# Mixture of experts after an adaptive layer norm, on one core: how the expert rows come back into token order

## The chip, the cores and the metric

The kernel runs on one core of a Trainium2 chip. The metric is the device time of one execution in microseconds (us), the median of several runs. Its engines are named as the profile names them: PE is TensorE (PEld its weight loads), DVE is VectorE, ACT is ScalarE, POOL is GpSimd and SP is SyncE; SPq, ACTq and POOLq are their sequencers, which issue DMAs.

## The reference, cut to what matters

The input x has 8 batches of 128 tokens with 128 features, float32. An adapter and a layer norm, chosen for each batch by a language number, make n from x. A router picks one of 8 experts for each of the 1024 tokens; the expert's result and that of a shared network are added to x:

```python
x0 = x
n = _L0_cond_ref(x, ids, W1, b1, W2, b2, gamma, beta)     # adapter, layer norm
logits = n @ router_w.T
top_idx, score = argmax(logits), sigmoid(max(logits))
xs = n * score[:, None]
h = silu(xs @ expert_gate[e]) * (xs @ expert_up[e])       # for each expert e, FF = 256
moe_out = sum over e of onehot[:, e] * (h @ expert_down[e])
sh = silu(n @ shared_gate) * (n @ shared_up) @ shared_down
out = x0 + moe_out + sh
```

## The kernel before, in words

Everything is float32 and tokens lie in tiles of 128 rows, one row per partition. The work runs in three stages, each engine with its own program, tied by semaphores.

First stage: adapter, layer norm and router over the 8 batches in two groups of 4. VectorE works out for each token a slot in a list that is sorted by expert (`find_slot`, line 854). Each expert has one home tile of 128 places, and 7 more tiles take what runs over; of these the first four (`RARE = 4`) are always worked on, the last three only if the data needs them (`rare_in_use`, line 183), which is not so with these inputs. ScalarE scales the rows by their score (line 642), and GpSimd scatters them with eight indirect DMAs, one per batch (line 341), into the scratch `slots_x` in device memory: 129 numbers per row, the last one being the token's own number. That scratch was filled before with rows whose number is `NO_TOKEN = 4 * T`. SyncE then loads the sorted tiles back into `slot_x` with nine DMAs (line 268).

Second stage, beside it: the shared network. VectorE adds its result to x, batch by batch (`residual`, line 798), which gives `r_rows`. SyncE stores them to the output with two DMAs, each for four batches (line 272), on its queue behind the nine loads.

Third stage, twelve tiles (`main`: four run-over tiles, then the eight experts). For each tile TensorE transposes it (line 539), ScalarE copies it (line 683), TensorE multiplies with the expert's gate and up weights (line 547 for the run-over tiles, line 551 for the others), ScalarE applies silu (line 699), VectorE multiplies (line 944), TensorE multiplies with the down weights (line 575), and VectorE copies the result to `y` (line 949). For each tile GpSimd then issues an indirect DMA (line 350, in `tiles_out`) that adds its 128 rows to the output at the rows given by the token numbers (`compute_op=ALU.add`). The number `NO_TOKEN` of an unused place is above the bound `T - 1`, and its row is dropped (`bounds_check`, `oob_is_err=False`). Since these DMAs add to rows that the stores of line 272 write, GpSimd first waits for both stores (`r_out`). The program ends when SyncE has seen all of them land (`main.y_out`).

The order on every engine is the order of the code. GpSimd's descriptors for indirect DMAs go on the DMA queue named software_dynamic (q0), those of SyncE and ScalarE on queues named hardware_dynamic (q1 and q10).

Of the kernel before, what the change touches and what calls it, by code (L numbers as in the profile page):

```python
# [6 lines left out]
P = 128  # L7
F32 = mybir.dt.float32
# [9 lines left out]
def adaln_moe_kernel(nc, x, ids, w1rw, w2b2, lang_vecs, shared_w, expert_w, out):  # L18
# [3 lines left out]
    S, B, H = x.shape  # L22
# [5 lines left out]
    T = B * S  # L28
    assert S == P and H == P and shared_w.shape[1] == 2 * FF + K2 * H
    GROUPS = 2  # L30
    GB = B // GROUPS
# [13 lines left out]
    out_rows = out.rearrange("b s h -> (b s) h")  # L45

    with ExitStack() as ctx:  # L47
        def sb(name, shape, dt=F32):
            return ctx.enter_context(nc.sbuf_tensor(name, shape, dt))

        def sem(name):
            return ctx.enter_context(nc.semaphore(name))
# [74 lines left out]
        r_rows = sb("r_rows", [P, B, H])  # L127
# [5 lines left out]
        y = sb("y", [P, TILES, H])  # L133

# [23 lines left out]
        fill_x, x_out, r_out = sem("fill_x"), sem("x_out"), sem("r_out")  # L158

        sg_ps, su_ps, sg_done, hs_done = sem("sg_ps"), sem("su_ps"), sem("sg_done"), sem("hs_done")  # L160
        sd_ps, r_done = sem("sd_ps"), sem("r_done")
# [15 lines left out]
        rare = Run("rare", list(range(E + RARE, TILES)))  # L177
# [70 lines left out]

        block = ctx.enter_context(nc.Block())

        @block.sync
        def _(sp):
# [17 lines left out]
            for g in range(GROUPS):  # L270
                sp.wait_ge(r_done, (g + 1) * GB)
                sp.dma_start(out[g * GB:(g + 1) * GB].rearrange("b s h -> s b h"), r_rows[:, g * GB:(g + 1) * GB, :]
                             ).then_inc(r_out, 16)
# [3 lines left out]
            sp.wait_ge(main.y_out, 16 * main.n)  # L277

        @block.gpsimd
        def _(pool):  # L280
# [64 lines left out]
            def tiles_out(run):  # L345
                pool.wait_ge(r_out, 16 * GROUPS)
                for i, tile in enumerate(run.tiles):
                    pool.wait_ge(slot_x_in[piece_of(tile)], 16)
                    pool.wait_ge(run.y_done, i + 1)
                    nc.gpsimd.indirect_dma_start(  # L350
                        out=out_rows,
                        out_offset=bass.IndirectOffsetOnAxis(ap=slot_x[:, tile, H:H + 1].bitcast(U32), axis=0),
                        in_=y[:, tile, :], in_offset=None, bounds_check=T - 1, oob_is_err=False,
                        compute_op=ALU.add).then_inc(run.y_out, 16)
# [246 lines left out]
        def _(act):  # L601
# [102 lines left out]
            with nc.scalar.If(rare_in_use(nc.scalar)):  # L704
                expert_tiles(rare)
                act.wait_ge(rare.eh_done, rare.n)
            expert_tiles(main)

        @block.vector
        def _(dve):  # L710
# [248 lines left out]
            expert_tiles(main)  # L959

# [33 lines left out]
```

## Time and profile before

| | us |
|---|---|
| median of 3 runs | 69.2 (68.46 to 69.24) |
| the profiled execution's own time | 68.22 |
| its span, first to last instruction | 66.4 |
| POOL busy | 30.5 |
| PE busy | 48.8 |
| DVE busy | 27.0 |
| ACT busy | 22.7 |

The span is what the trace shows. The execution's own time has 1.82 us more, which lie outside it. The profile's busy time is an instruction's time on its engine; for an indirect DMA on POOL that is the time in which its descriptors are made, not the time in which its rows move. What a DMA takes from the start of its issue until it has landed stands in the rows "to landing". Times in the trace are counted in us from the start of the span.

### The profile page before, as it was taken

Reading aid. Unit: us, or ns where it says so; the run is one execution under the profiler, and the core shown is the slowest. Engines: PE = TensorE matmul, PEld = TensorE weight load, DVE = VectorE, ACT = ScalarE, POOL = GpSimd, SP = SyncE. Lnnn points to the kernel's source line nnn. Section 1 sums busy time; section 2 is a strip of 40 time slices with the busy share of each in tenths; the row PEclk is TensorE's granted clock in tenths of the full one; section 3 lists DMA queues with packets and bytes.
Section 4 is the critical chain, followed back from the end, with each engine's and each line's share of the span. In section 5 each row is a group of like instructions: output and inputs, shape, how many; then the busy total and the mean of one; then the engine's idle time right before and its main releaser. Section 6 shows DMA issues by size and latency. Waiting matters only on the chain.

```text
span 66.4 us, 1128 instructions
## 1 busy us (share of the span) xinstructions
PE 48.8 (74%) x312; PEld 36.4 (55%) x312; DVE 27.0 (41%) x119; ACT 22.7 (34%) x65; POOL 30.5 (46%) x51
## 2 busy tenths in 40 slices
PE   3999999999898967999629999999999840000000
PEld 1376888676647424479414469999999730000000
DVE  2602364576881789747500433353333530000000
ACT  0640256568778081330023555533344200000000
POOL 4002950000138658860000000898888888898820
PEclk9999999999999999999999999999999999855555
DMA  0870899999899841111269590043421003424140
GB/s 0 255 267 4 141 336 163 114 176 239 370 402 427 363 149 62 47 40 45 77 158 238 126 314 11 0 40 33 40 27 7 5 4 24 40 22 40 9 37 2
DMA packets 7994, 8.05 MB, mean 121 GB/s; under 512 B 1161, under 2 KB 7187, under 8 KB 7732
## 3 DMA queue, kind: packets, MB, share of 16 engines
q1 hardware_dynamic: 5820, 6.74, 38.2%
q0 software_dynamic: 1984, 1.06, 11.9%
q10 hardware_dynamic: 184, 0.18, 1.0%
q8 instruction: 3, 0.05, 0.3%
q14 instruction: 3, 0.02, 0.1%
HBM read 5.40 MB, written 2.83 MB: 124 GB/s over the span
## 4 chain that ended last, share of the span: by engine, by line
PE 52%; POOL 10%; ACT 9%; DVE 7%; issue 7%; DMA 7%; POOLq 3%; ACTq 0%
PE bank L551 11%; POOL out_dram L350 9%; PE bank L575 8%; PE bank L547 6%; PE bank L365 6%; DMA slots_x<-x_rows,slot 4%; PE bank L379 4%; PE bank L395 3%; PE bank L389 3%; POOLq L47 3%; ACT x_rows L642 3%; DMA slot_x<-slots_x 3%; PE bank L373 2%; PE bank L539 2%; ACT L663 2%
## 5 line engine op out<-in xcount | busy, mean ns | idle before, releaser
L350 POOL DMA_INDIRECT out_dram<-y,slot_x x12 | 18.8, 1564 | 15.1 <-DVE y L949 12.4
L341 POOL DMA_INDIRECT slots_x<-x_rows,slot x8 | 7.9, 990 | 4.2 <-ACT x_rows L642 1.8
L448 PE MATMUL bank<-nT,sh_w 128*128 128x512 f32 (+1 forms) x20 | 8.3, 527 | 0.9 <-DVE hs L793 0.9
L944 DVE TENSOR_TENSOR eh<-eg,bank 128x256 f32<-128x256 f32 x12 | 5.0, 418 | 9.1 <-ACT eg L699 9.1
L551 PE MATMUL bank<-exT,ex_w 128*128 128x128 f32 x64 | 8.5, 275 | 0.0
L551 PEld LDWEIGHTS bank<-exT,ex_w 128*128 128x128 f32 x64 | 7.8, 192 | 0.0
L699 ACT ACTIVATE eg<-bank 128x256 f32<-128x256 f32 x12 | 4.6, 383 | 9.0 <-PE bank L551 6.5
L949 DVE COPY y<-bank 128x128 f32<-128x128 f32 x12 | 3.4, 287 | 4.8 <-PE bank L575 4.8
L575 PE MATMUL bank<-ex_w,eh 128*128 128x128 f32 x32 | 5.0, 278 | 0.5 <-DVE eh L944 0.5
L683 ACT ACTIVATE exT<-bank 128x128 f32<-128x128 f32 x12 | 3.2, 273 | 5.8 <-PE bank L539 5.8
L365 PE MATMUL bank<-warm 128*128 128x512 bf16 x11 | 4.4, 538 | 1.1 <-DVE eps L712 1.1
L448 PEld LDWEIGHTS bank<-nT,sh_w 128*128 128x128 f32 x20 | 3.3, 190 | 2.9 <-DVE hs L793 1.6
L575 PEld LDWEIGHTS bank<-ex_w,eh 128*128 128x128 f32 x32 | 4.2, 192 | 0.7 <-DVE eh L944 0.7
L547 PE MATMUL bank<-ex_w,exT 128*128 x8 | 4.2, 618 | 0.3 <-ACT exT L683 0.3
L539 PE MATMUL bank<-ident,slot_x 128*128 128x128 f32 x12 | 3.2, 277 | 1.5 <-issue 1.5
L463 PEld LDWEIGHTS bank<-sh_w,hs 128*128 128x128 f32 x32 | 3.7, 192 | 0.5 <-issue 0.5
L333 POOL TENSOR_SCALAR score<-half_tanh 128x4 f32<-128x4 f32 x1 | 0.2, 192 | 8.1 <-ACT half_tanh L630 8.1
L463 PE MATMUL bank<-sh_w,hs 128*128 128x128 f32 x32 | 3.7, 275 | 0.0
L637 ACT ACTIVATE sg<-bank 128x512 f32<-128x512 f32 x4 | 2.4, 601 | 2.5 <-PE bank L448 2.5
L793 DVE TENSOR_TENSOR hs<-sg,bank 128x512 f32<-128x512 f32 x4 | 2.6, 682 | 1.2 <-PE bank L448 1.0
L610 ACT ACTIVATE hT<-bank,params 32x128 f32<-32x128 f32 x6 | 1.7, 347 | 3.9 <-PE bank L389 3.9
L642 ACT ACTIVATE x_rows<-bank,score 128x128 f32<-128x128 f32 x8 | 2.3, 368 | 2.1 <-DVE score L891 1.7
(125 smaller groups left out, 74.7 us busy)
## 6 DMA issues: line engine op xcount, KB each, us to landing
ex_w<-in_expert_w_dram SPq DMA_DIRECT2D x2, 1536.0 KB
slots_x<-empty_row SPq DMA_DIRECT2D x1, 967.5 KB, 11.3
slot_x<-slots_x SPq DMA_DIRECT2D x4, 129.0 KB, 3.8
x_tok<-in_x_dram SPq DMA_DIRECT2D x2, 256.0 KB, 3.6
out_dram<-r_rows SPq DMA_DIRECT2D x2, 256.0 KB, 3.2
sh_w<-in_shared_w_dram SPq DMA_DIRECT2D x1, 384.0 KB, 3.5
slot_x<-slots_x SPq DMA_DIRECT2D x4, 64.5 KB, 1.9
slot_x<-slots_x SPq DMA_DIRECT2D x1, 193.5 KB, 4.0
```

What stands on the lines that cost most here:

```text
L341: nc.gpsimd.indirect_dma_start(out=slots_x, out_offset=bass.IndirectOffsetOnAxis(ap=slot[:, b:b + 1], axis=0), in_=x_rows[:, b, :], in_off ...
L350: nc.gpsimd.indirect_dma_start(out=out_rows, out_offset=bass.IndirectOffsetOnAxis(ap=slot_x[:, tile, H:H + 1].bitcast(U32), axis=0), in_=y ...
L365: nc.tensor.matmul(bank[bk][:, 0:blocks * P], warm[:], warm[:].unsqueeze(1).to_broadcast([P, blocks, P]), start=True, stop=True)
L448: last = nc.tensor.matmul(bank[SH_BANKS[k][u]][:, first * S:end * S], sh_w[:, u * FF + k * P:u * FF + (k + 1) * P], nT[:, g * GB + first:g ...
L463: last = nc.tensor.matmul(sh_y_place(b), hs[:, k, b * S:(b + 1) * S], sh_w[:, 2 * FF + k * H:2 * FF + (k + 1) * H], start=(k == 0), stop=( ...
L539: nc.tensor.transpose(bank[EX_X[i % 2]][:, 0:P], slot_x[:, run.tiles[i], 0:H], ident[:]).then_inc(run.exT_ps, 1)
L547: last = nc.tensor.matmul(bank[EX_GU[i % 2]][:], exT[:, i % 2, :], ex_w[:, bass.ds(expert[i], 1), 0:2 * FF], start=True, stop=True)
L551: last = nc.tensor.matmul(bank[EX_GU[i % 2]][:, k * P:(k + 1) * P], ex_w[:, expert[i], k * P:(k + 1) * P], exT[:, i % 2, :], start=True, s ...
L575: last = nc.tensor.matmul(bank[EX_Y[i % 2]][:, 0:H], hidden, ex_w[:, bass.ds(expert[i], 1), 2 * FF + k * H:2 * FF + (k + 1) * H], start=(k ...
L642: nc.scalar.activation(x_rows[:, b, 0:H], bank[N_ROWS][:, (b % GB) * H:(b % GB + 1) * H], ACT.Copy, scale=score[:, b:b + 1]).then_inc(scal ...
L699: nc.scalar.activation(eg[:, i % 2, :], bank[EX_GU[i % 2]][:, 0:FF], ACT.Silu).then_inc(run.eg_done, 1)
L944: nc.vector.tensor_tensor(eh[:, i % 3, :], eg[:, i % 2, :], bank[EX_GU[i % 2]][:, FF:2 * FF], ALU.mult).then_inc(run.eh_done, 1)
```

## The change

The twelve indirect DMAs no longer add to the output: they write the expert rows plainly into a second scratch, `y_tok`, in token order. They keep the bound, and no longer wait for the stores of line 272, which are gone. When all twelve have landed, `y_tok` is loaded back into `y_back` by four plain DMAs of two batches each, the first and third from SyncE, the second and fourth from ScalarE. VectorE adds `y_back` to `r_rows` in four additions, and four plain DMAs, again by turns from SyncE and ScalarE, store the sums.

```diff
     slots_x = nc.dram_tensor("slots_x", (TILES * P, ROW), F32, kind="Internal").ap()
-    out_rows = out.rearrange("b s h -> (b s) h")
+    y_tok = nc.dram_tensor("y_tok", (T, H), F32, kind="Internal").ap()
+    RETURNS = 4
...
+        def batches(i):
+            return slice(i * B // RETURNS, (i + 1) * B // RETURNS)
+
+        def load_back(engine, i):
+            engine.dma_start(y_back[:, batches(i), :], y_tok.rearrange("(b s) h -> s b h", s=S)[:, batches(i), :]
+                             ).then_inc(y_in[i], 16)
+
+        def store_out(engine, i):
+            engine.wait_ge(out_added, i + 1)
+            engine.dma_start(out[batches(i)].rearrange("b s h -> s b h"), out_sb[:, batches(i), :]
+                             ).then_inc(out_stored, 16)
...
         def _(sp):
...
-            for g in range(GROUPS):
-                sp.wait_ge(r_done, (g + 1) * GB)
-                sp.dma_start(out[g * GB:(g + 1) * GB].rearrange("b s h -> s b h"), r_rows[:, g * GB:(g + 1) * GB, :]
-                             ).then_inc(r_out, 16)
...
             sp.wait_ge(main.y_out, 16 * main.n)
+            for i in range(0, RETURNS, 2):
+                load_back(sp, i)
+            for i in range(0, RETURNS, 2):
+                store_out(sp, i)
+            sp.wait_ge(out_stored, 16 * RETURNS)
...
             def tiles_out(run):
-                pool.wait_ge(r_out, 16 * GROUPS)
                 for i, tile in enumerate(run.tiles):
                     pool.wait_ge(slot_x_in[piece_of(tile)], 16)
                     pool.wait_ge(run.y_done, i + 1)
                     nc.gpsimd.indirect_dma_start(
-                        out=out_rows,
+                        out=y_tok,
                         out_offset=bass.IndirectOffsetOnAxis(ap=slot_x[:, tile, H:H + 1].bitcast(U32), axis=0),
-                        in_=y[:, tile, :], in_offset=None, bounds_check=T - 1, oob_is_err=False,
-                        compute_op=ALU.add).then_inc(run.y_out, 16)
+                        in_=y[:, tile, :], in_offset=None, bounds_check=T - 1, oob_is_err=False
+                        ).then_inc(run.y_out, 16)
...
             expert_tiles(main)
+            act.wait_ge(main.y_out, 16 * main.n)
+            for i in range(1, RETURNS, 2):
+                load_back(act, i)
+            for i in range(1, RETURNS, 2):
+                store_out(act, i)
...
             expert_tiles(main)
+            for i in range(RETURNS):
+                dve.wait_ge(y_in[i], 16)
+                dve.wait_ge(r_done, B)
+                nc.vector.tensor_tensor(out_sb[:, batches(i), :], r_rows[:, batches(i), :], y_back[:, batches(i), :],
+                                        ALU.add).then_inc(out_added, 1)
```

In the built program these are the rows that change place. First SyncE's queue from the loads of the sorted tiles to its end, before:

```order
L268 DMA slot_x<-slots_x 128x2x129 x4
L268 DMA slot_x<-slots_x 128x3x129
L272 DMA out_dram<-r_rows 128x4x128 [waits r_done] x2
L183 TENSOR_LOAD over_size [waits over_ex_done,slot_x_in8]
L183 ISA x2
L275 COMPARE_AND_BRANCH
L275 UNCONDITIONAL_BRANCH [waits rare_y_out]
L47 UNCONDITIONAL_BRANCH [waits main_y_out]
```

And the same stretch of SyncE's queue now:

```order
L285 DMA slot_x<-slots_x 128x2x129 x4
L285 DMA slot_x<-slots_x 128x3x129
L188 TENSOR_LOAD over_size [waits over_ex_done,slot_x_in8]
L188 ISA x2
L288 COMPARE_AND_BRANCH
L288 UNCONDITIONAL_BRANCH [waits rare_y_out]
L258 DMA y_back<-y_tok 128x2x128 [waits main_y_out]
L258 DMA y_back<-y_tok 128x2x128
L263 DMA out_dram<-out_sb 128x2x128 [waits out_added] x2
L48 UNCONDITIONAL_BRANCH [waits out_stored]
```

The two stores of `r_rows` behind the loads are gone; two loads and two stores stand at the end, behind the wait for all scatters. ScalarE's queue has the same four at its end, behind its last activation. VectorE's end before, with the last products and copies of the expert tiles:

```order
L949 COPY y<-bank 128x128 [waits main_y_ps]
L944 TENSOR_TENSOR eh<-eg,bank 128x256 [waits main_y_ps,main_eg_done]
L949 COPY y<-bank 128x128 [waits main_y_ps]
L944 TENSOR_TENSOR eh<-eg,bank 128x256 [waits main_y_ps,main_eg_done]
L949 COPY y<-bank 128x128 [waits main_y_ps] x2
L47 UNCONDITIONAL_BRANCH
```

And VectorE's end now:

```order
L972 COPY y<-bank 128x128 [waits main_y_ps]
L967 TENSOR_TENSOR eh<-eg,bank 128x256 [waits main_y_ps,main_eg_done]
L972 COPY y<-bank 128x128 [waits main_y_ps] x2
L986 TENSOR_TENSOR out_sb<-r_rows,y_back 128x256 [waits r_done,y_in0]
L986 TENSOR_TENSOR out_sb<-r_rows,y_back 128x256 [waits r_done,y_in1]
L986 TENSOR_TENSOR out_sb<-r_rows,y_back 128x256 [waits r_done,y_in2]
L986 TENSOR_TENSOR out_sb<-r_rows,y_back 128x256 [waits r_done,y_in3]
L48 UNCONDITIONAL_BRANCH
```

The four additions stand behind the last copy, each behind its own load. GpSimd's queue keeps its order; only the wait for `r_out` at its first expert tile is gone.

## Rows read from the trace of the kernel before

**Rows 1.** The page, part 4: the chain that ended last, by engine and line.
```profile
PE 52%; POOL 10%; ACT 9%; DVE 7%; issue 7%; DMA 7%; POOLq 3%; ACTq 0%
PE bank L551 11%; POOL out_dram L350 9%; PE bank L575 8%; PE bank L547 6%; PE bank L365 6%; DMA slots_x<-x_rows,slot 4%; PE bank L379 4%; PE bank L395 3%; PE bank L389 3%; POOLq L47 3%; ACT x_rows L642 3%; DMA slot_x<-slots_x 3%; PE bank L373 2%; PE bank L539 2%; ACT L663 2%
```

**Rows 2.** The chain's last pieces: start us, us, what.
```profile
54.48 1.55 POOL out_dram L350
...
60.06 1.56 POOL out_dram L350
61.62 0.30 issue
61.93 1.55 POOL out_dram L350
```

**Rows 3.** POOL in time: start, us, engine, line, operation [idle before <-releaser].
```profile
24.88 0.95 POOL L341 DMA_INDIRECT slots_x<-x_rows,slot  x1 [0.62 <-DVE slot L854]
26.14 0.96 POOL L341 DMA_INDIRECT slots_x<-x_rows,slot  x1 [0.30 <-issue]
...
41.37 1.61 POOL L350 DMA_INDIRECT out_dram<-y,slot_x  x1 [11.74 <-DVE y L949]
...
61.93 1.55 POOL L350 DMA_INDIRECT out_dram<-y,slot_x  x1 [0.30 <-issue]
```

**Rows 4.** VectorE in time, 38 to 55 us; the first and last two of twelve copies.
```profile
38.84 0.29 DVE L949 COPY y<-bank 128x128 f32<-128x128 f32 x1 [1.07 <-PE bank L575]
...
52.81 0.42 DVE L944 TENSOR_TENSOR eh<-eg,bank 128x256 f32<-128x256 f32 x1 [0.72 <-ACT eg L699]
53.15 0.28 DVE L949 COPY y<-bank 128x128 f32<-128x128 f32 x1
...
54.03 0.29 DVE L949 COPY y<-bank 128x128 f32<-128x128 f32 x1 [0.60 <-PE bank L575]
```

**Rows 5.** Line 272: ns min/median/max, first and last start, and landing.
```profile
L272 SPq DMA_DIRECT2D out_dram<-r_rows x2: 488/498/507, 36.6 to 37.2; - x2
...
DMA to landing us min/median/max: 3.1/3.2/3.4
```

**Rows 6.** The DMA from 63 to 67 us, 40 slices of 0.1 us.
```profile
DMA  0000000000897999630000000000000000000000
...
out_dram<-y,slot_x POOLq DMA_INDIRECT x1, 3.3
```

**Rows 7.** The waits of SP's queue: in total, times, longest.
```profile
SPq L47 <- PEq L47: 0.9, 1, 0.9
```

**Rows 8.** VectorE in time: the slot numbers of the two groups.
```profile
18.09 0.18 DVE L854 TENSOR_REDUCE slot<-at_last 128x4 uint32<-128x32 f32 x1
...
24.42 0.19 DVE L854 TENSOR_REDUCE slot<-at_last 128x4 uint32<-128x32 f32 x1
```

**Rows 9.** The two groups of indirect DMAs: ns min/median/max, first and last start.
```profile
L341 POOL DMA_INDIRECT slots_x<-x_rows,slot x8: 952/958/1206, 19.3 to 28.7; - x8
...
L350 POOL DMA_INDIRECT out_dram<-y,slot_x x12: 1555/1559/1609, 41.4 to 61.9; - x12
```

**Rows 10.** DMA queue q0, 18 to 31.5 us, then 41 to 67: packets, MB, share.
```profile
q0 software_dynamic: 256, 0.53, 11.5%
...
q0 software_dynamic: 1728, 0.53, 24.4%
```

**Rows 11.** The chain from 28.67 us: last plain scatter, first load back.
```profile
28.67 2.61 DMA slots_x<-x_rows,slot
...
31.29 1.72 DMA slot_x<-slots_x
```

**Rows 12.** Stretches: busy of PE, PEld, DVE, ACT, POOL; PEclk, DMA share, GB/s.
```profile
34.00:36.60 2.60, 2.23 (x7) 0.94 (x7) 0.22 (x1) 1.00 (x4) 0.00 (x0) 1.00 0.81 210
...
37.40:39.00 1.60, 1.60 (x11) 1.12 (x11) 0.53 (x2) 0.86 (x3) 0.00 (x0) 1.00 1.05 287
```

**Rows 13.** The page, part 6: DMA issues, KB each, median us to landing.
```profile
slot_x<-slots_x SPq DMA_DIRECT2D x4, 129.0 KB, 3.8
```

More of the change, by code:

```diff
@@ L133, in adaln_moe_kernel @@
         y = sb("y", [P, TILES, H])
+        y_back = sb("y_back", [P, B, H])
+        out_sb = sb("out_sb", [P, B, H])
         x_in = [sem(f"x_in{i}") for i in range(GROUPS)]
@@ L157, in adaln_moe_kernel @@
         n_ps, scaled = sem("n_ps"), sem("scaled")
-        fill_x, x_out, r_out = sem("fill_x"), sem("x_out"), sem("r_out")
+        fill_x, x_out = sem("fill_x"), sem("x_out")
+        y_in = [sem(f"y_in{i}") for i in range(RETURNS)]
+        out_added, out_stored = sem("out_added"), sem("out_stored")
         sg_ps, su_ps, sg_done, hs_done = sem("sg_ps"), sem("su_ps"), sem("sg_done"), sem("hs_done")
@@ L706, in _ @@
                 act.wait_ge(rare.eh_done, rare.n)
+                act.wait_ge(rare.y_out, 16 * rare.n)
             expert_tiles(main)
+            act.wait_ge(main.y_out, 16 * main.n)
[3 more added lines that the diff above has]
+                store_out(act, i)
         @block.vector
```

## Prediction

> **What bounds the kernel now.** I read the page first, then the chain of waits, then the order in time on GpSimd (POOL) and VectorE (DVE) in the last third, then the DMA by stretches. The profiled execution took 68.22 us; its span is 66.4 us, so 1.82 us lie outside. The median of the runs shown is 69.2 us, 0.98 us above the profiled one; all sums are made against 68.22 and moved to the median at the end.
>
> The page's chain puts only 9% on the scatter [rows 1], which understates it. At the end of the span the chain holds nothing but GpSimd [rows 2]: each 1.56 us scatter is followed by 0.30 us of issue, and no releaser other than GpSimd itself stands between. GpSimd's own rows show when this begins [rows 3]: the first of the twelve starts at 41.37, the last at 61.93. Eleven steps in 20.56 us are 1.87 us each. VectorE had the first expert tile in SBUF at 38.84 + 0.29 = 39.13 and the last at 54.03 + 0.29 = 54.32 [rows 4]. So the expert tiles arrive over 15.2 us, GpSimd spends 22.1 us on them (41.37 to 63.48), and TensorE, ScalarE and VectorE are idle after 54.3. The bound of the last 25 us is the scatter's descriptor work on GpSimd, at 1.87 us per tile, and it starts 2.2 us after its first tile is there.
>
> Why it starts late: two stores of the residual rows (line 272) begin at 36.6 and 37.2 and land 3.1 and 3.4 us after their issue [rows 5], the second near 40.6; GpSimd waits for both before it may add to the output.
>
> After the last scatter's issue at 61.93 the DMA engines move its rows between 64.0 and 64.9, and it lands 3.3 us after its start [rows 6], at about 65.2. The remaining 1.2 us to 66.4 are the closing of the program; the wait of 0.9 us in it stands in SyncE's waits [rows 7].
>
> **What the change removes, and what that is worth.**
> Step 1, the wait for the residual stores. They are gone, and so the first scatter waits for its tile alone (39.13). A wait-bound scatter in the first group began 0.27 us after its release (the tile's slot numbers end at 24.42 + 0.19 = 24.61, the scatter starts at 24.88 [rows 3, 8]). After a long idle time it may be later, up to 1.0 us: the very first one starts at 19.3 [rows 9], its slot numbers end at 18.09 + 0.18 = 18.27. I take 39.4 to 40.1 for the first start, 1.3 to 2.0 us earlier than now.
>
> Step 2, the scatter itself. The trace holds a plain indirect scatter on the same engine: the eight of line 341 take 0.952 to 1.206 us, median 0.958 [rows 9]; their gap where nothing holds them is the same 0.30 us. They differ from line 350 in two things, not one: they have no addition, and no check of the index against a bound. The change takes away only the addition; the bound stays, since unused places of a tile carry an index beyond the output. So the price of the new scatter has two ends: 0.96 us (all of the extra 0.60 us is the addition's) and 1.56 us (all is the bound's). The packets show that the descriptors differ in form too: 256 packets for the eight plain scatters, 32 each, against 1728 for the twelve others, 144 each [rows 10]. Which of the two does that, no row says. I take 0.96 us, since an addition needs the row that is there to be read as well as the row that is sent, a second thing to describe for each of the 128 rows, while the comparison is one operation on each index; and since the twelve durations are alike (1555 to 1609 ns [rows 9]), although 1024 rows in 1536 places leave some tiles with many unused places, where a check that fails would have work of its own. It is a choice, and the largest risk here.
>
> With 0.96 + 0.30 = 1.26 us per step GpSimd keeps up: eleven intervals over 14.9 us are 1.36 us on average. Only the last ones matter. The eleventh tile is ready at 53.15 + 0.28 = 53.43, its scatter starts at 53.70; the twelfth is ready at 54.32, and its scatter starts at the later of 54.32 + 0.27 and 53.70 + 1.26, which is 54.96. The last start moves from 61.93 to 54.96: 7.0 us earlier. What is late next is the expert stage itself, which this change does not touch.
>
> Step 3, landing. SyncE's first load from the first scratch starts at 31.29, 2.61 us after the last plain scatter started at 28.67 [rows 11]; the adding one takes 3.3 [rows 6]. I take 2.6, so the scatters have landed at 57.6 instead of 65.2. Steps 1 to 3 save 7.6 us.
>
> **What the change adds, all of it on the path.** Nothing hides the following; every engine is idle by then. SyncE and ScalarE issue two loads each and later two stores each; behind the waiting instruction on either engine stand only these and the end. The wait of ScalarE for the scatters comes after its last activation and delays nobody.
> Loads: the first load of the first scratch (64.5 KB) landed 1.72 us after its start [rows 11]; its DMA work begins about 0.8 us after the start (the rest of the 1.72 being 0.25 to move 64.5 KB and the landing), as I read it. The four loads are 512 KB. Rows of that scratch moved at 210 GB/s with the DMA engines 81% busy [rows 12], about 260 GB/s at full use: 256 KB need 1.0 us, 512 KB 2.0 us. So the first pair, one from each engine, lands at 0.8 + 1.0 + 0.2 = 2.0 us, the second pair at 3.0 us.
> Additions: four of 128x256. The nearest row is line 944, 0.42 us each [rows 4]. Two run from 2.0 to 2.85, two from 3.0 to 3.9.
> Stores: the last, 128 KB, is issued at 3.9. A store of 256 KB next to another of the same size took 3.1 us [rows 5]; for 128 KB with its neighbours mostly done I take 2.1 us (0.8 to begin, 0.45 to move at 287 GB/s [rows 12], the rest to be confirmed). Sum: 3.9 + 2.1 = 6.0 us.
> Bounds of this term: below, loads all down at 2.3, one addition after them (0.4), a store of 1.7 as the quickest load: 4.4. Above, the slowest rows throughout: loads 3.8 [rows 13], additions 2 x 0.42, store 3.4: 8.1 us.
> The Trainium skill, DMA: Bandwidth & Descriptors (section Anatomy of one DMA), gives about 2.0 us plus the bytes at 436 GB/s for a DMA that GpSimd issues. Used for these it would be an estimate of 3.2 for the loads and 2.3 for the last store, with 0.85 of additions 6.35 in all, 0.35 more than mine; the trace's 1.72 us for a small load is below its fixed part.
>
> Dropping the two 256 KB stores at 36.6 also leaves the DMA engines free while the last pieces of the tiles are loaded. The page's chain holds only 3% for those loads [rows 1], which is the one first load of 1.72 us; none of the later ones is waited for, so I cost it at nothing.
>
> **Sum.** Last scatter start 54.96, landing 2.6 (57.6), return 6.0 (63.6), closing 1.2 (64.8), outside 1.82: 66.6 us against 68.22, 1.6 us or 2.4% faster. On the median of 69.2 that is 67.6 us. About 2% is what a measurement of this kernel can tell from no change.
>
> **The rivals.**
> A, slower: the bound's check is what costs. The scatter stays at 1.56 us, the step at 1.87. The point from which it decides: the sum is above 68.22 where the last scatter starts after 56.4, that is from a step of 1.52 or a scatter of 1.22 us on, and above it by 2% from a scatter of 1.33 us on. For it: line 350 is the only group with a bound, and the packet count could come from it as well. Against it: the argument above. The first scatter starts at 39.4 to 40.1, the last 20.5 later at 59.9 to 60.6, landing 3.2, return 6.0, closing 1.2: span 70.3 to 71.0, own time 72.1 to 72.8, 73.1 to 73.8 on the median, some 6% slower. Where the step grows past 1.5 us GpSimd falls behind the tiles, and from there each 0.1 us of a scatter costs 1.1 us.
> B, in between: addition and bound share the extra. At 1.25 us the step is 1.55, the last start 39.7 + 17.05 = 56.75, landing 2.9: 1.8 + 0.3 us worse than forecast, 69.7 on the median: no difference.
> C, the return is dear: the read of rows just written, or the two queues, take 8 us instead of 6 at a fast scatter: 69.6 us, no difference or barely slower.
> D, the return is cheap: 4.8 us, 66.4 us.
>
> **How the numbers follow.** Forecast 0.48, A 0.27, B 0.14, C 0.07, D 0.04. The forecast's own range is 66.4 to 68.8: a first start, a landing and a return each off by half a microsecond. Of its 0.48 I give 0.31 to faster than 2% (below 67.8), 0.17 to within. With D and a little of B, faster is 0.37. Within 2%: 0.17 of the forecast, 0.07 of B, 0.03 of C: 0.27. Slower: A and the rest of B and C: 0.36. The range must reach into A, since leaving A out would leave out more than 2 in 10: 66.3 to 73.2 us.
>
> **What would show it.** Right: scatters of 0.95 to 1.05 us on GpSimd, each put down to VectorE's copy and not to issue, the last started near 55; four loads landing 2 to 3 us later, additions of 0.42 us, the last store landing 6 us after the last scatter landed. Wrong: scatters of 1.5 us in unbroken steps after 54.3 (rival A), or over 7 us between the landing of the scatters and that of the stores (C). If the packets per scatter fall from 144 to 32, the addition made their form; if they stay, the bound did.

## The result, and the profile after

The changed kernel takes 68.4 us (median of 20 runs) where the kernel before took 68.86 us beside it (20 runs): a ratio of 0.994, 95% interval 0.992 to 0.997. That is 0.6% faster, which counts as no difference at 2%; the forecast was 2.4%. Its profiled execution took 68.52 us, its span is 66.7 us, so 1.82 us lie outside as before. (Some executions of any of these kernels take longer than the rest, so a ratio is taken over those within 1.5% of the kernel's quickest, a median over all.)

The groups of the page that answer to [rows 1] and [rows 9], first the chain by lines, then the scatters and the new additions:

```profile
PE bank L568 9%; PE bank L592 6%; PE bank L564 6%; PE bank L382 6%; DMA y_back<-y_tok 5%; PE bank L396 4%; DMA slots_x<-x_rows,slot 4%; DMA y_tok<-y,slot_x 3%; PE bank L412 3%; POOL y_tok L367 3%; PE bank L406 3%; DMA slot_x<-slots_x 3%; POOL slots_x L359 2%; PE bank L390 2%; PE bank L556 2%
...
L367 POOL DMA_INDIRECT y_tok<-y,slot_x x12 | 11.8, 984 | 16.5 <-DVE y L972 13.3
...
L986 DVE TENSOR_TENSOR out_sb<-r_rows,y_back 128x256 f32<-128x256 f32 x4 | 1.6, 423 | 6.6 <-DMA y_back<-y_tok 6.6
```

The scatter fell from 1.56 to 0.98 us, and the idle time before it is now put down to VectorE's copy: through most of the stretch GpSimd waits for tiles. A new 6.6 us stands before the additions, VectorE's wait for the loads back. The line numbers moved: 367 was 350, 972 was 949, 568 was 551, 716 was 699.

The packets of the twelve scatters, 41 to 60 us (against 1728 in [rows 10]):

```profile
q0 software_dynamic: 384, 0.53, 8.7%
```

384 are 32 per scatter, as the eight scatters of the first group have. They carry the same bound as before; so it was the addition that made both the price and the form of the descriptors, and not the bound.

GpSimd in time, as in [rows 3]: start, duration, and in brackets the idle time before.

```profile
25.69 0.97 POOL L359 DMA_INDIRECT slots_x<-x_rows,slot  x1 [1.18 <-DVE slot L877]
...
40.79 1.00 POOL L367 DMA_INDIRECT y_tok<-y,slot_x  x1 [10.32 <-DVE y L972]
42.41 0.99 POOL L367 DMA_INDIRECT y_tok<-y,slot_x  x1 [0.62 <-issue]
...
49.72 0.98 POOL L367 DMA_INDIRECT y_tok<-y,slot_x  x1 [0.43 <-issue]
52.66 0.98 POOL L367 DMA_INDIRECT y_tok<-y,slot_x  x1 [1.95 <-DVE y L972]
...
57.81 0.98 POOL L367 DMA_INDIRECT y_tok<-y,slot_x  x1 [0.30 <-issue]
```

And VectorE's copies of the expert tiles, as in [rows 4]: the first, the seventh to tenth, the last.

```profile
39.65 0.29 DVE L972 COPY y<-bank 128x128 f32<-128x128 f32 x1 [1.07 <-PE bank L592]
...
48.60 0.29 DVE L972 COPY y<-bank 128x128 f32<-128x128 f32 x1 [0.25 <-PE bank L592]
51.53 0.29 DVE L972 COPY y<-bank 128x128 f32<-128x128 f32 x1 [0.61 <-remote]
52.38 0.28 DVE L972 COPY y<-bank 128x128 f32<-128x128 f32 x1
53.38 0.28 DVE L972 COPY y<-bank 128x128 f32<-128x128 f32 x1
...
55.80 0.29 DVE L972 COPY y<-bank 128x128 f32<-128x128 f32 x1 [0.60 <-PE bank L592]
```

Here is the surprise. The last scatter was forecast to start at 54.96; it starts at 57.81, mostly since the copies are late. The first ends at 39.94 instead of 39.13, the last at 56.09 instead of 54.32. Two places make this. The fifth scatter of the first group starts at 25.69 instead of 24.88. 0.23 us of that lie before this group (its first scatter starts at 19.49, before it was 19.26), and 0.5 us are a gap on VectorE: its row at 23.78 needs products of line 505 that TensorE had finished at 23.30 (22.98 for 0.32 us).

```profile
23.78 0.19 DVE L867 TENSOR_TENSOR place_hot<-bank,hot 128x32 f32<-128x32 f32 x1 [0.51 <-PE bank L505]
```

From the last scatter of the first group to the first copy the time is the same in both traces (29.50 to 39.65 and 28.67 to 38.84), so the late first copy comes from this place alone. The other place is between the copies at 48.60 and 51.53, 2.9 us instead of 1.45. ScalarE shows it, and the row of TensorE that it waits for stands below:

```profile
47.51 0.38 ACT L716 ACTIVATE eg<-bank 128x256 f32<-128x256 f32 x1 [0.90 <-PE bank L568]
...
50.09 0.38 ACT L716 ACTIVATE eg<-bank 128x256 f32<-128x256 f32 x1 [2.02 <-PE bank L568]
51.62 0.38 ACT L716 ACTIVATE eg<-bank 128x256 f32<-128x256 f32 x1 [0.99 <-PE bank L568]
```

```profile
47.87 1.06 PE L568 MATMUL bank<-exT,ex_w 128*128 128x128 f32 x8
```

TensorE had finished the products for the second of ScalarE's rows at 48.93 (47.87 and 1.06 us). ScalarE starts at 50.09, 1.1 us late, and the view puts it down to TensorE only because it names the last semaphore that rose. Nothing that the profile shows held ScalarE. TensorE's own line had to wait for it in turn, so the interval from the first copy to the last is 16.15 us, where it was 15.19. Behind the gap three tiles come 0.85 and 1.0 us apart, faster than GpSimd's step of 1.29 us, and GpSimd's last five starts, from 52.66 on, are unbroken steps.

The end, as [rows 2] and [rows 11] had it, from the last scatter on, and under it the landing of the loads (line 258) and of the stores (line 263):

```profile
57.81 2.26 DMA y_tok<-y,slot_x
60.06 0.02 issue
60.08 0.36 SPq L258
60.45 0.05 issue
60.49 3.05 DMA y_back<-y_tok
```

```profile
DMA to landing us min/median/max: 2.3/2.9/3.1
...
DMA to landing us min/median/max: 1.9/1.9/1.9
```

The scatters land 2.26 us after the last start, the loads back 2.3 to 3.1 us after theirs, and the last store starts at 64.36 and lands at 66.3: 6.2 us for the whole return, forecast as 6.0. The span closes 0.45 us later, not 1.2.

### The profile page after: what moved, and what is told of

Same layout as the page of the kernel before. It is cut to its first block, busy times and chain, and to the rows that moved or that the text cites. A ratio compares the mean times of both kernels' runs of the same rounds, so it can differ in the third digit from the quotient of the medians.

```text
span 66.7 us, 1142 instructions
## 1 busy us (share of the span) xinstructions
PE 49.6 (74%) x312; PEld 36.5 (55%) x312; DVE 28.6 (43%) x123; ACT 22.7 (34%) x65; POOL 23.6 (35%) x51
## 3 DMA queue, kind: packets, MB, share of 16 engines
q0 software_dynamic: 640, 1.06, 4.8%
## 4 chain that ended last, share of the span: by engine, by line
PE 46%; DMA 15%; issue 14%; ACT 8%; POOL 6%; DVE 4%; POOLq 1%; DVEq 1%; SPq 1%; ACTq 0%
PE bank L568 9%; PE bank L592 6%; PE bank L564 6%; PE bank L382 6%; DMA y_back<-y_tok 5%; PE bank L396 4%; DMA slots_x<-x_rows,slot 4%; DMA y_tok<-y,slot_x 3%; PE bank L412 3%; POOL y_tok L367 3%; PE bank L406 3%; DMA slot_x<-slots_x 3%; POOL slots_x L359 2%; PE bank L390 2%; PE bank L556 2%
## 5 line engine op out<-in xcount | busy, mean ns | idle before, releaser
L367 POOL DMA_INDIRECT y_tok<-y,slot_x x12 | 11.8, 984 | 16.5 <-DVE y L972 13.3
L986 DVE TENSOR_TENSOR out_sb<-r_rows,y_back 128x256 f32<-128x256 f32 x4 | 1.6, 423 | 6.6 <-DMA y_back<-y_tok 6.6
```

What stands on the lines that cost most here:

```text
L367: nc.gpsimd.indirect_dma_start(out=y_tok, out_offset=bass.IndirectOffsetOnAxis(ap=slot_x[:, tile, H:H + 1].bitcast(U32), axis=0), in_=y[:, ...
```

## The experiments

Every kernel was timed beside the kernel before on the same chip; ratios are to it. Four chips were used: a first for the next four runs, a second for the two tries at ScalarE's idle wait and for the returns "two parts" and "no return at all", a third for the changed kernel beside its two variants and for the single accumulating DMA, a fourth for the two runs under "A fourth chip" and for the smaller first loads.

**The scatter alone.** In the kernel before:

```diff
-                        in_=y[:, tile, :], in_offset=None, bounds_check=T - 1, oob_is_err=False,
-                        compute_op=ALU.add).then_inc(run.y_out, 16)
+                        in_=y[:, tile, :], in_offset=None, bounds_check=T - 1, oob_is_err=False
+                        ).then_inc(run.y_out, 16)
```

> The kernel before with the addition taken out of the twelve scatters and nothing else changed: they write the bare expert rows over the residual rows, so the residual and the shared result are missing from the rows. It prices the scatter alone. Theory (the addition was the whole 0.6 us): 0.98 us per scatter, 32 packets each, first start 41.4 (still held by the residual stores), last start 55.6 (twelfth copy at 54.3, then 0.84 us or the step of 1.28), landed at 57.8, own time about 60.9 us, ratio 0.89. Rival 1 (the addition is not it): 1.56 us and a ratio of 1.00. Rival 2 (a plain scatter beside the expert tiles slows them): the twelfth copy ends at 56 as in the changed kernel, time about 62.5 us, ratio 0.91.

Ratio 0.924 (0.915 to 0.933), its two quickest executions 63.1 and 63.4 us. The scatters take 0.98 us, so the addition is the whole 0.6 us (rival 1 falls). It gains 5.2 us of the 7.6 expected, and why the rest is missing is not shown: its only trace is of its longest execution (67.1 us). That trace has VectorE's gap (fifth scatter at 25.10, 1.13 us after the fourth ended), and in it the copies take 19.7 us from first to last. The time is nearer to rival 2 (0.91), but the run with one accumulating DMA at the end, below, has the same plain scatters into the output beside the same expert tiles, and there the copies take 15.19 us, as before: the scatters as such do not slow them.

**The return taken away.** In the changed kernel the loads back, additions and stores are left out:

```diff
             sp.wait_ge(main.y_out, 16 * main.n)
-            for i in range(0, RETURNS, 2):
-                load_back(sp, i)
-            for i in range(0, RETURNS, 2):
-                store_out(sp, i)
-            sp.wait_ge(out_stored, 16 * RETURNS)
```

(and the same on ScalarE, and VectorE's four additions)

> The changed kernel without loads back, additions and final stores: the output is never written. It prices the return. Theory A (the changed program's expert stage is late by 1.8 us in every execution, whatever stands at its end): the twelfth copy ends near 56, last scatter 57.8, own time about 63.1 us, so the return costs 5.3 us. Rival B (the lateness belongs to the instructions that were added at the ends of ScalarE and VectorE, or to that one execution): the twelfth copy ends near 54.5 to 55, own time 60.9 to 61.5, and the return costs 7 us.

Ratio 0.910 (0.904 to 0.917), 62.3 us. The first and last copy, and the last scatter:

```profile
39.15 0.29 DVE L962 COPY y<-bank 128x128 f32<-128x128 f32 x1 [1.07 <-PE bank L587]
...
55.26 0.29 DVE L962 COPY y<-bank 128x128 f32<-128x128 f32 x1 [0.60 <-PE bank L587]
...
57.27 0.98 POOL L362 DMA_INDIRECT y_tok<-y,slot_x  x1 [0.31 <-issue]
```

The last scatter starts at 57.27 and the span ends at 60.6, 3.3 us later. In the changed kernel on the same chip (next run) these are 57.07 and 65.8, 8.7 us. So the return costs 5.4 us net of the closing that it shortens; forecast were 6.0 with the closing left as it was. The copies' interval is 16.11 us: ScalarE's gap is there without the instructions at the ends of ScalarE and VectorE.

**The changed kernel again.**

> The changed kernel itself once more, for its trace. Two gaps in which no semaphore held the engine stood in its first trace: 0.46 us on VectorE at 23.3 and 1.1 us on ScalarE at 49. Theory A (they belong to this program): both are there again within 0.1 us, the twelfth copy ends at 55.9 to 56.2, ratio 0.995. Rival B (chance of one execution): they are gone, and the span is 65 us.

Its profiled execution took 67.62 us. Both gaps are there: the fifth scatter of the first group 1.12 us after the fourth, interval 16.07 us. Rival B falls; they are no chance of one execution. The twelfth copy ends at 55.35 and not at 55.9 or later, since here the first scatter of the first group starts at 18.95, 0.3 us before that of the kernel before. Its four executions (67.62 to 69.97 us) are too scattered for a ratio.

**The kernel before with its residual stores earlier.**

```diff
+            for g in range(GROUPS):
+                act.wait_ge(r_done, (g + 1) * GB)
+                act.dma_start(out[g * GB:(g + 1) * GB].rearrange("b s h -> s b h"), r_rows[:, g * GB:(g + 1) * GB, :]
+                              ).then_inc(r_out, 16)
```

(on ScalarE ahead of its expert tiles, and gone from SyncE)

> The kernel before with the two residual stores issued from ScalarE's queue as soon as the rows are there, ahead of its expert work, where they stood behind nine loads on SyncE's queue. Theory: the first scatter no longer waits and starts 0.84 us after its tile, at 40.0, all twelve steps of 1.87 follow, last start 60.5, own time about 66.8 us, ratio 0.98. Rival (the stores move beside the loads of the sorted tiles and delay the first of them, or hold ScalarE): the first copy of a tile is later by as much, ratio 0.99 to 1.01.

Ratio 0.987 (0.978 to 0.997). ScalarE's two issues, the first copy and the first scatter:

```profile
31.88 2.23 ACTq L675 DMA_DIRECT2D out_dram<-r_rows  x2
...
39.94 0.29 DVE L949 COPY y<-bank 128x128 f32<-128x128 f32 x1 [1.07 <-PE bank L571]
...
41.17 1.61 POOL L346 DMA_INDIRECT out_dram<-y,slot_x  x1 [10.76 <-DVE y L949]
```

The wait for the stores is gone: the scatter starts 0.94 us after its copy, and before it was 2.2. The first copy comes 1.1 us later than in the first trace. 0.8 of that lies before the last scatter of the first group (29.45, was 28.67), with VectorE's gap in it (fifth scatter at 25.66, 1.13 us after the fourth ended); only 0.3 us is left for what the rival had, the stores beside the loads of the tiles. Removing a wait, without touching the 1.87 us step behind it, is worth 1.3%. The copies' interval here is 15.19 us: this program has no gap on ScalarE, on the chip on which the two before have it.

**Does ScalarE's idle wait make the gap?** The only difference between ScalarE's programs before and in the run without the return is a wait in a branch that is not taken. First added to the kernel before:

```diff
                 act.wait_ge(rare.eh_done, rare.n)
+                act.wait_ge(rare.y_out, 16 * rare.n)
             expert_tiles(main)
```

> The kernel before with one added wait: in ScalarE's program, inside the branch for the rare tiles that is not taken, it waits for the rare tiles' scatters, as the changed kernel does there. Nothing that is executed changes. Theory A (ScalarE's gap of 1.1 us in the eighth activation of line 699 comes from where its instructions lie, and this one shifts them): the interval from the first to the twelfth copy of y grows from 15.2 to 16.1 us, and the total stays within 0.5% since GpSimd's steps of 1.87 us hide it. Rival B (the gap comes from something else in the changed kernel: the plain scatters, the longer ends): the interval stays at 15.2 us.

Ratio 1.001 (0.997 to 1.006), interval 15.19 us: no gap. Then taken out of the changed kernel:

> The changed kernel without that one wait in ScalarE's branch that is not taken (the case in which the rare tiles are needed is then not protected). Theory A: the interval of the copies falls from 16.1 to 15.2 us, three tiles no longer pile up behind it, the last scatter starts 0.84 us after the last copy or one step behind, some 1.3 us earlier than now, and the time falls from 68.2 to 67.0 us, ratio 0.975. Rival B: interval 16.1 us, ratio 0.995.

Ratio 0.970 (0.964 to 0.976), 65.9 us, interval 15.20 us. That looked like theory A at its best and was not: on this chip no kernel had either gap, and the changed kernel itself was not among them. It had to stand beside its variants:

> The changed kernel a third time, now in one call and on one chip with the kernel without ScalarE's idle wait. In the last call no kernel showed the gap on ScalarE, the kernel before with the added wait among them, so the gap may belong to the chip or to the call. Theory A (it belongs to the changed program): interval of the copies 16.1 us, gap of 2.0 us before the eighth activation, ratio 0.99 to 1.00. Rival C (it belonged to the chip or the call): interval 15.2 us and a ratio of 0.97, the same as its neighbour here.

> The changed kernel without the wait in ScalarE's branch that is not taken, again. Theory A: interval 15.2 us, ratio 0.965 to 0.975, 1.3 to 2 us below its neighbour. Rival C: same time as its neighbour within 0.5%.

```diff
                 act.wait_ge(rare.y_out, 16 * rare.n)
+                act.wait_ge(rare.y_done, rare.n)
```

> The changed kernel with a second wait that is never executed beside the first. Theory A1 (the number of instructions ahead of ScalarE's expert work decides whether it has to wait for its next ones): the gap moves or goes, interval anywhere from 15.2 to 16.1 us but not at the same activation. Theory A2 (any added instruction does it): gap at the eighth activation again, interval 16.1 us or more.

Ratios 0.983 (0.977 to 0.988), 0.978 (0.968 to 0.989) and 0.978 (0.967 to 0.989); intervals 15.19, 15.20 and 15.19 us. With the wait, without it or with two of them the kernels cannot be told apart, and the changed kernel, on a third chip, is 1.8% faster than before rather than 0.6%. The wait by itself makes no gap. Whether ScalarE's gap is there goes with the chip (or with how the program was placed on it), and not with it alone, as the early stores showed. Nor is this chip free of pauses: in the kernel with two waits, and in the one with a single accumulating DMA, TensorE's weight loads stand still for 0.63 us at 19 us with nothing that the profile shows to hold them, and the fifth scatter of the first group starts 1.46 and 1.55 us after the fourth has ended.

**A fourth chip.** It was still open whether the two kernels differ on a chip with the gaps.

> The changed kernel once more, on whichever chip comes. If its trace has VectorE's gap (the fifth scatter of the first group more than 1.0 us after the fourth ended, 0.6 without it), this chip is of the first kind: then the interval of the copies is 16.1 us and the ratio 0.99 to 1.00. If not, the interval is 15.2 us and the ratio 0.975 to 0.985.

> The kernel without ScalarE's idle wait beside it. On a chip with VectorE's gap: theory A (the program decides where ScalarE has to pause) 15.2 us between first and last copy and a time 1 us or more below its neighbour; rival C (the chip alone) 16.1 us and the same time. On a chip without it: the same as its neighbour within 0.5%, and A against C stays open.

Ratios 0.985 (0.978 to 0.993) and 0.969 (0.961 to 0.978), both intervals 15.19 us. Again a chip without gaps, so that question stays open. The difference between the two has another place. TensorE from 36 to 38 us, first the changed kernel, then its neighbour (busy times, then granted clock, DMA share, GB/s):

```profile
36.00:38.00 2.00, 2.00 (x6) 1.03 (x5) 0.50 (x2) 0.59 (x3) 0.00 (x0) 0.50 0.31 80
```

```profile
36.00:38.00 2.00, 2.00 (x8) 0.82 (x7) 0.84 (x2) 1.45 (x5) 0.00 (x0) 1.00 0.53 128
```

The granted clock was 0.50 there, the lower of its two levels (1.2 GHz), from about 34.8 to 38.2 us, and the same pair of products of line 564 took 1.92 us where it takes 1.02. The first copy came 11.5 us after the start of the last scatter of the first group, the neighbour's 10.2: the dip costs 1.4 us. What sets it off is not shown. TensorE had been idle for 1.5 us up to 33.28, but the neighbour was idle as long up to 34.01 and kept its clock. On these two chips the executions of the changed kernel fall into two groups: seven of 65.7 to 66.4 us with a mean granted clock of 0.942 to 0.950, and nine of 66.7 to 67.1 us with 0.921 to 0.931. One trace of the second group on each chip has the dip; for the others it is read from the mean clock. The neighbour has 3 such executions of 10 on these chips and none of 4 on the second chip; that is too few to tell from chance.

The end of the neighbour's trace is the forecast with neither gap nor dip in its way; last copy, last scatter, and the chain:

```profile
54.03 0.29 DVE L971 COPY y<-bank 128x128 f32<-128x128 f32 x1 [0.60 <-PE bank L592]
...
55.55 0.98 POOL L367 DMA_INDIRECT y_tok<-y,slot_x  x1 [0.31 <-issue]
```

```profile
55.55 2.25 DMA y_tok<-y,slot_x
57.80 0.02 issue
57.82 0.36 SPq L258
58.18 0.05 issue
58.23 2.90 DMA y_back<-y_tok
```

Its copies end at 54.32, to the hundredth where [rows 4] had them. The last scatter starts at 55.55 (forecast 54.96), one unbroken step of 1.29 us behind the eleventh at 54.26, which starts 0.83 us after its own copy; it has landed at 57.80 (57.6), and the span is 64.3 us (64.8), the time 66.13 (66.6).

**Other forms of the return.** Two parts of four batches (`RETURNS = 2`, without ScalarE's idle wait):

> The kernel of the run before last (changed kernel without ScalarE's idle wait) with the return in two parts of four batches instead of four parts of two: one load, one store on each engine, two additions of 128x512. Theory (the return is fixed latency plus 0.5 MB each way at about 300 GB/s, cut finely it overlaps): both loads land together 2.8 us after their start, two additions of 0.8 us, the last store of 256 KB is issued at 4.5 and takes 2.3: 6.8 us in place of 6.1, so 0.7 us slower than four parts. Rival (issuing DMAs is what costs): no slower, since two issues of 0.45 us per engine fall away.

Ratio 0.985 (0.981 to 0.990), against 0.970 for four parts on the same chip, 1.1 us slower. The landing of its loads and of its stores:

```profile
DMA to landing us min/median/max: 3.2/3.4/3.5
...
DMA to landing us min/median/max: 2.3/2.5/2.6
```

Loads started at 58.97, the last store at 63.51 and landed 2.6 us later: 7.1 us for the return, where four parts take 6.1 to 6.2. So the rival falls: two issues fewer on each engine did not pay, since the larger loads and stores land later and the additions begin later.

One accumulating DMA at the end (plain scatters straight into the output, the residual rows stored to a scratch `r_tok` meanwhile):

```diff
+            pool.wait_ge(r_out, 16 * GROUPS)
+            pool.wait_ge(main.y_out, 16 * main.n)
+            nc.gpsimd.dma_start(out_rows.rearrange("(p j) h -> p (j h)", p=P), r_tok.rearrange("(p j) h -> p (j h)", p=P),
+                                accum_op=ALU.add, max_dma_last_dim=4096).then_inc(r_added, 16)
```

> Another return: the kernel before with plain scatters straight into the output, the residual rows stored to a scratch meanwhile, and at the end one accumulating DMA from GpSimd that adds the scratch to the output in 128 rows of 4 KB. Theory (one trip instead of two): last scatter starts near 55.5, landed 2.3 later, then 1.6 us of descriptors and about 3 us to move and land: 4.5 us in place of 6.0, ratio 0.95. Rival (each row of 1024 numbers is cut and the descriptors cost as in line 350, or the adding is slow): 7 us or more, ratio 0.98 or above.

Ratio 0.989 (0.980 to 0.998). Its start, and its landing:

```profile
59.18 0.98 POOL L363 DMA_DIRECT2D out_dram<-r_tok  x1 [1.87 <-DMA out_dram<-y,slot_x]
```

```profile
out_dram<-r_tok POOLq DMA_DIRECT2D x1, 512.0 KB, 5.5
```

Its descriptors cost 0.98 us, not 1.6, but it lands 5.5 us after its start, at 64.7, and that is 6.1 us after the scatters had landed at 58.6, where 4.5 were expected: no better than two trips.

**No return at all.** The residual rows are sorted too, while GpSimd is idle, and added before the scatter:

```diff
+            for b in range(B):
+                pool.wait_ge(r_done, b + 1)
+                nc.gpsimd.indirect_dma_start(
+                    out=slots_r, out_offset=bass.IndirectOffsetOnAxis(ap=slot[:, b:b + 1], axis=0),
+                    in_=r_rows[:, b, :], in_offset=None).then_inc(rs_out, 16)
...
+                    op = nc.vector.tensor_tensor(y[:, tile, :], source, slot_r[:, tile, :], ALU.add)
```

> Another way to the same output, built on the kernel before: the residual rows are scattered into expert order by eight more plain scatters, in the ten microseconds in which GpSimd is idle between the two scatter groups, and loaded back by four DMAs; VectorE adds them to the expert rows (the first four tiles after their copy, the others straight from PSUM in place of the copy), and the twelve plain scatters then write the finished rows to the output. No wait for residual stores, no addition in a DMA, no return. Theory: the residual scatters start at 30 and end at 40, landed at 41.2, first rows loaded at 43.3, output scatters from 44.5 in steps of 1.28 (three or more of them waiting for VectorE at first), last start 58 to 59, landed 2.3 later, closing 1.2: span 61.5 to 62.5, own time 63.3 to 64.3, ratio 0.93. Rival (the additions or the extra loads hold VectorE and so TensorE): the copies' stage is longer by 1 to 3 us and the ratio is 0.95 to 0.98.

Ratio 0.970 (0.963 to 0.977). The last residual scatter, the loads of the sorted rows, the first addition, the first and the last output scatter:

```profile
39.76 0.97 POOL L376 DMA_INDIRECT slots_r<-r_rows,slot  x1 [0.30 <-issue]
...
42.03 2.01 SPq L300 DMA_DIRECT2D slot_r<-slots_r  x4
...
45.13 0.29 DVE L989 TENSOR_TENSOR y<-y,slot_r 128x128 f32<-128x128 f32 x1 [0.57 <-DMA slot_r<-slots_r]
...
46.34 1.00 POOL L385 DMA_INDIRECT out_dram<-y,slot_x  x1 [5.61 <-DVE y L989]
...
60.64 0.98 POOL L385 DMA_INDIRECT out_dram<-y,slot_x  x1 [0.31 <-issue]
```

The ratio was to be 0.93. GpSimd is the bound again: eleven steps of 1.30 us behind a first start at 46.34, 1.8 us later than expected. The residual scatters had landed at 42.0 and not at 41.2, and the first load took 3.0 us to land instead of 2.1. The last start is then 60.64, where 58 to 59 was expected, and this kernel's time is 2.2 us above its span where the others' is 1.8; that was not looked into. The expert tiles are not slower (from the first copy to the twelfth row that takes a tile from PSUM 15.19 us), so the rival falls, although the measured ratio is in its range. Smaller first loads:

> The kernel that sorts the residual rows, with their way back in six loads, the first four of two tiles each in the order in which they are wanted, where it was four tiles at once. Its chain from the second run on: residual scatters landed, first load, first addition, then twelve output scatters in unbroken steps of 1.287 us. Theory: the first load lands 2.2 us after its start instead of 2.9, the first output scatter starts 0.7 us earlier, every later one too: ratio 0.96 where it was 0.97. Rival (the later pieces now come too late for the order of the scatters): a gap among the first four output scatters, and no gain.

```profile
45.60 1.00 POOL L385 DMA_INDIRECT out_dram<-y,slot_x  x1 [4.94 <-DVE y L989]
```

The first output scatter is 0.7 us earlier as expected, and the profiled time 65.7 instead of 66.55, but the ratio is 0.970 (0.965 to 0.975), the same, where 0.96 was expected. The two stood on different chips, and intervals this wide do not resolve 0.7 us. Its median of 65.85 us against 68.06 is the lowest of any kernel here that leaves nothing out.

## Why the prediction was wrong

The direction was right, and so was the mechanism of what is removed and of what is added. The size was 2.4% where 0.6% was measured, and rival A, the largest chance against the forecast, was wrong altogether. The measured 68.4 us lies inside the stated range, but that says little: the range was drawn wide to reach into rival A.

Right: the addition is the scatter's extra 0.6 us (0.98 us measured, 0.96 taken), and the packets fell from 144 to 32. The choice between the two prices was a choice, as the prediction says, and its argument, a second thing to describe for each row, was not tested; the runs show the price and not its reason. The first scatter waits for its tile alone. The loads land 2.3 to 3.1 us after their start (2.0 and 3.0 from the first start were taken), an addition takes 0.42 us, the last store 1.9 us (2.1), the return 6.1 to 6.2 us (6.0).

Three smaller terms were off and nearly cancel, which is luck. A wait-bound scatter was taken to start 0.27 us after its release, from the one row of the first group; for an expert tile it is 0.84 us (39.94 to 40.79 in the changed kernel, 0.84 again at the next three). That puts 0.6 us on the end of the chain, through the eleventh scatter and the step behind it. The kernel before had such a row at the same place: its stores landed near 40.6 and the scatter that waited for them started at 41.37. Against it stand minus 0.35 for the landing (2.26, 2.6 taken) and minus 0.75 for the closing, which I had as 1.2 us by subtraction and which is 0.4 to 0.45 in the kernels whose last DMA to land is one of the stores from SyncE and ScalarE; where one of GpSimd's lands last it is 1.1 to 1.4 (also with the return taken away, and with the single accumulating DMA). On a chip without the gaps all of it gives 66.13 us against a forecast of 66.6. (Two figures of the prediction are off by its own terms, with no weight: rival A's point is a last start of 56.6 and not 56.4, and the upper bound of the return adds up to 8.0.)

The step that failed is the sentence "What is late next is the expert stage itself, which this change does not touch". It was costed at nothing and its times were taken from one execution. In the two traces of the changed kernel that have ScalarE's gap (on the chip of the first comparison and on that of the first experiments) it makes the last copy 0.96 and 0.88 us later, and the tiles that pile up behind it cost GpSimd a further 0.5 us: 1.72 us lie between the last copy's end and the last scatter in both, 1.23 in the trace with no gap. In the first of them another 0.8 us comes from VectorE's gap and what lay before it; in the second this is only 0.15, since that trace began its first group earlier. In numbers, for the first: 0.8 + 0.96 + 0.5 for the late tiles, + 0.6 - 0.35 + 0.2 - 0.75 for the rest, is 2.0 us, which takes the span of 64.8 that was forecast to the 66.7 measured, within 0.1.

Between the medians the miss is smaller, 1.2 us: by the forecast's 2.4% the 68.86 us of the kernel before become 67.2, and 68.4 was measured. The forecast rests on a trace of 68.22 us, 0.64 below that median. Two variants of the kernel before, on the chip of the first experiments, have VectorE's gap too. If it is in the usual executions of both kernels, the 0.8 cancels between them and the other terms, 1.2 us, are the miss; no trace of the kernel before was taken that could show this.

In the kernel before, a delay of the copies after the first would cost little, since twelve steps of 1.87 us lie over it: its twelfth copy ends 7.6 us before its scatter starts, its eighth, the one that ScalarE's gap hits, 5.3 us (49.19 to 54.48). This is read from the order of the waits; no trace of a kernel with the slow scatter has ScalarE's gap. The change took that cover away, so it exposed delays of the expert tiles that had been free. Without ScalarE's gap the ratio was 0.983 and 0.985, with TensorE's dip in clock in nine of sixteen executions; whether the kernel before loses as much by such a dip was not looked at.

What stays open: why ScalarE starts 1.1 us late on some chips and in some programs. An idle wait in its branch does not make it on a chip without the gap; on a chip with it, the kernel without the wait was never run. A transfer on the instruction queue of 0.02 MB lies beside the gap in two of three traces with it, but after it in the third, and equally in traces without a gap, so it explains nothing by itself; that an engine waits for its next instructions is a rival that these runs do not rule out.

## What to carry to other kernels

Ask of an accumulating scatter what its descriptors cost: here the addition made each 0.58 us dearer for 128 rows. Against that the trip back must be paid once, with nothing to hide it: 6.2 us for 0.5 MB each way in four overlapping parts, a microsecond more in two. An estimate from these two prices is that plain scatters pay only where more than ten of them stand in a row on GpSimd, and then only until the tiles themselves become the bound. When a change removes the engine that bounds a stretch, the times of whatever bounds it next are not those of one trace: price its disturbances, which had been free until then, and look at that trace more than once. Where a wait and not a backlog sets the start of a GpSimd DMA, take the delay from a wait-bound row of the same program place, not from the shortest one.

## What the runs showed of the hardware that was not expected

- A plain scatter that checks 128 indices against a bound costs 0.98 us, one without the check 0.97 us; the check costs next to nothing here. An adding scatter is 1.56 us, with 144 packets where the plain one has 32.
- The engine gaps of 0.5 us (VectorE) and 1.1 us (ScalarE), in which nothing that the profile shows held them, came again from execution to execution (interval of the copies 16.15, 16.11 and 16.07 us in three traces of the changed kernel and the one without its return) and are absent from all eleven traces of three other chips (15.19 or 15.20 us). On one chip VectorE's gap stood in all four traces, ScalarE's in the two with the changed program and not in the kernel with early stores (15.19 us).
- GpSimd starts the plain scatter of an expert tile 0.84 us after the copy it waits for has ended (the adding one 0.94 us in the kernel with early stores), where after another DMA of its own it takes 0.30 us. In the first group the scatter that waited for its slot numbers started after 0.27 us. Why the two differ was not looked into.
- A plain accumulating DMA of 0.5 MB in rows of 4 KB, issued from GpSimd, takes 0.98 us on GpSimd and lands 5.5 us after its start.
- The closing of the program after the last landing took 0.4 us where that was a store from SyncE or ScalarE, and 1.1 to 1.4 us where it was a DMA from GpSimd.
